# The second layer's attention moved two batches behind the first layer's, with the order of all engines written out in tables

## The reference

```python
x = x + _L0_attn_ref(_layernorm(x), ...)   # 16 heads of 8, softmax attention
x = x + _L0_ffn_ref(_layernorm(x), ...)    # silu(gate) * up, hidden 384, then down
x = x + _L1_attn_ref(_layernorm(x), ...)   # 16 heads of 8, RMS-normed q and k
x = x + _L1_ffn_ref(_layernorm(x), ...)    # base linear + 8 gated experts of rank 8
...
scores = jax.nn.softmax(jnp.einsum('bhse,bhte->bhst', q, k) * scale, axis=-1)
att = jnp.einsum('bhst,bhte->bhse', scores, v)
```

## Time and profile before

| | |
|---|---|
| median of 3 runs | 2082.71 us (2080.16 to 2085.62) |
| the profiled execution, own time | 2080.51 us |
| its span | 2078.7 us |
| TensorE busy | 1806.1 us (87%) |
| VectorE busy | 1601.2 us (77%) |
| ScalarE busy | 1431.7 us (69%) |
| GpSimd busy | 433.7 us (21%) |

### The profile page before, as it was taken

How to read it: one execution, slowest core, us unless ns; L and a number is a source line. 1 busy time by engine, 2 the same in 40 slices (tenths; PEclk the granted TensorE clock), 3 DMA queues, 4 the chain that set the end, 5 groups by cost and what they waited for, 6 DMA issues and landing times.

```text
span 2078.7 us, 32069 instructions
## 1 busy us (share of the span) xinstructions
PE 1806.1 (87%) x10958; PEld 664.0 (32%) x10958; DVE 1601.2 (77%) x3593; ACT 1431.7 (69%) x2921; POOL 433.7 (21%) x570
## 2 busy tenths in 40 slices
PE   4958998999899999999899998989899989999685
PEld 1232333333233333333233333323333332323322
DVE  3537888887788887887888888788888878787371
ACT  2716777776767777786867777776777868676543
POOL 2112121121213122121312212131211312120300
PEclk9957999999899999999999999999999999999867
DMA  5202214050411405041230504032050504121110
GB/s 112 67 17 79 72 39 123 18 144 17 122 40 48 116 20 140 18 123 38 79 88 18 144 17 132 26 108 58 25 137 18 144 17 119 38 60 36 42 42 17
DMA packets 162644, 141.34 MB, mean 68 GB/s; under 512 B 38761, under 2 KB 144050, under 8 KB 162482
## 3 DMA queue, kind: packets, MB, share of 16 engines
q1 hardware_dynamic: 162482, 139.29, 25.2%
HBM read 77.38 MB, written 55.57 MB: 64 GB/s over the span
## 4 chain that ended last, share of the span: by engine, by line
PE 48%; DVE 17%; ACT 13%; DMA 11%; issue 5%; POOL 4%; SPq 3%; DVEq 0%; ACTq 0%; POOLq 0%
PE ps L1127 16%; DVE neg_max L853 10%; PE ps L1112 9%; ACT probs L647 7%; PE ps L1148 6%; PE ps L1102 5%; PE ps L1078 4%; DMA k_stack<-k_rows 3%; DMA rden_all<-rden_rows 3%; PE ps L1191 2%; PE ps L1153 2%; PE ps L1141 2%; DMA k_rows<-kp 2%; DMA rden_rows<-rden 1%; DVE bn L830 1%
## 5 line engine op out<-in xcount | busy, mean ns | idle before, releaser
L853 DVE TENSOR_REDUCE neg_max<-ps 128x1 f32<-128x512 f32 x2048 | 1318.2, 683 | 159.6 <-PE ps L1102 151.4
L647 ACT ACTIVATE probs<-ps 128x512 f32<-128x512 f32 x2048 | 1093.7, 599 | 296.0 <-PE ps L1112 291.5
L1102 PE MATMUL ps<-k_stack,q_stack 48*128 48x512 bf16 x2048 | 700.2, 400 | 80.1 <-DVE neg_max L853 40.1
L1112 PE MATMUL ps<-q_stack,k_stack 50*128 50x512 bf16 x2048 | 654.8, 390 | 64.4 <-ACT probs L647 58.3
L1127 PE MATMUL ps<-probs,v_aug 128*32 128x512 f32 x4096 | 561.8, 621 | 2.5
L1112 PEld LDWEIGHTS ps<-q_stack,k_stack 50*128 50x128 bf16 x2048 | 150.5, 95 | 505.2 <-ACT probs L647 329.8
L1102 PEld LDWEIGHTS ps<-k_stack,q_stack 48*128 48x128 bf16 x2048 | 157.0, 94 | 284.7 <-DVE neg_max L853 220.3
L551 POOL TENSOR_TENSOR o_raw<-o_raw,rden_all 128x512 f32<-128x512 f32 x64 | 81.6, 1275 | 545.8 <-DMA rden_all<-rden_rows 545.8
L1127 PEld LDWEIGHTS ps<-probs,v_aug 128*32 128x32 f32 x4096 | 82.0, 108 | 138.3 <-issue 91.9
L653 ACT ACTIVATE xn<-x,shift,rstd 128x128 f32<-128x128 f32 x192 | 80.6, 486 | 53.0 <-POOL shift L534 53.0
L568 POOL TENSOR_TENSOR ht<-up,gs 128x512 f32<-128x512 f32 x48 | 61.0, 1271 | 254.1 <-ACT up L628 254.1
(11 more groups left out here) (103 smaller groups left out, 1524.6 us busy)
## 6 DMA issues: line engine op xcount, KB each, us to landing
q_stack<-q_rows SPq DMA_DIRECT2D x128, 192.0 KB, 3.8
k_stack<-k_rows SPq DMA_DIRECT2D x128, 192.0 KB, 4.9
rden_all<-rden_rows SPq DMA_DIRECT2D x64, 256.0 KB
q_rows<-qp SPq DMA_DIRECT2D x32, 384.0 KB, 3.3
k_rows<-kp SPq DMA_DIRECT2D x32, 384.0 KB, 3.0
q_rows<-qp SPq DMA_DIRECT2D x32, 256.0 KB, 3.4
k_rows<-kp SPq DMA_DIRECT2D x32, 256.0 KB, 3.2
x_in<-in_L_attn_x SPq DMA_DIRECT2D x16, 256.0 KB, 2.9
```

Source lines behind the costliest of these rows:

```text
L647: act.activation(probs[:, u % RING, :], ps[:, bank_of(l, u), :], ACT.Exp).then_inc(exps, 1)
L853: dve.tensor_reduce(neg_max[l][:, pair // 2, col:col + 1], ps[:, BANKS + bank_of(l, n), :], AX.X, ALU.max, negate=True).then_inc(max_taken, 1)
L1102: pe.matmul(ps[:, BANKS + bank_of(l, m), :], q_stack[l][row:row + KROWS, pair, tok:tok + 128], k_stack[l][row:row + KROWS, pair, :], start ...
L1112: pe.matmul(ps[:, bank_of(l, u), :], k_stack[l][row:row + AROWS, pair, tok:tok + 128], q_stack[l][row:row + AROWS, pair, :], start=True, s ...
```

## The change

`SLOTS` with its X and Y slots is gone. The attentions stand in a list, `ATTENDS`, with no empty place between them, and layer 1 is two batches behind layer 0 instead of one: (0,0), (0,1), (0,2), (1,0), (0,3), (1,1), ... (0,15), (1,13), (1,14), (1,15). Their places are called slots 0 to 31 below. Each engine has a table of half steps for its pieces, relative to a slot, and `GROUPS` says for every batch at which slot a group starts and by how much it is shifted. In the middle of the kernel M1 of batch b stands beside (1,b-1), 16 half steps ahead of where it stood in its slot; since (0,b) is then three slots back, `pr0` has far more than one slot between the end of its attention and itself. M2 stands 8 half steps ahead in its slot. E stands where it stood.

With this the order at the two ends is another one: M1 of batch 0 stands beside (0,1), M2 of batch 0 beside (0,2); M1 of batches 13, 14 and 15 stand beside (1,12), (0,15) and (1,13); P0 of the first batches is packed closer (`P0_fast`); for batches 14 and 15 of layer 1 the second half of the stack is read at half step 63 (`H1_tail`), since the attention before it is of the same layer and reads the stack until then. The same holds for (0,1) and (0,2) at the start.

Buffers follow: `v_aug`, `res` of layer 1 and `o_raw` of layer 0 become double, `rden_all` is shared by the layers, and the ring of probabilities has 12 tiles instead of 16. The `v_aug` buffers are cleared by GpSimd ahead of the loop instead of by VectorE. A piece of several matmuls is now issued as one loop; it stood at one half step before, too.

```diff
-X_PE = ((1, "xt0"), (3, "q0"), (4, "m01"), (5, "k0"), (7, "qt"), (8, "kt"), (11, "pr1"), (12, "m02"), (14, "v1"),
-        (19, "xt3"), (20, "m03"), (21, "rt"), (27, "ct"), (28, "m10"), (29, "out"))
-SLOTS = [("Y", -1)] + [(k, i) for i in range(BATCH + 2) for k in "XY" if (k, i) != ("Y", BATCH + 1)]
-RING = 16
+RING = 12
+ATTENDS = [(0, 0), (0, 1)] + [a for b in range(2, BATCH) for a in ((0, b), (1, b - 2))] + [(1, BATCH - 2), (1, BATCH - 1)]
+PE_AT = {"A": {"m0": -7, "m1": 9, "m2": 25, "m3": 41},
+         "P0": {"xt0": 3, "q0": 7, "k0": 11}, "P0_fast": {"xt0": 3, "q0": 5, "k0": 7}, "V0": {"v0": 15},
...
+         "M2": {"qt": 15, "kt": 17, "v1": 29},
+         "E": {"pr1": 23, "xt3": 39, "rt": 43, "ct": 55, "out": 59}}
...
+M1_EARLY = -16
+M2_EARLY = -8
+GROUPS = []
+for n, (layer, b) in enumerate(ATTENDS):
+    GROUPS.append(("A", (layer, b), n, 0))
+for b in range(1, BATCH):
+    early = b < 3
+    GROUPS.append(("P0_fast" if early else "P0", b, SLOT_OF[0, b - 1], 2 if 2 <= b <= 3 else 0))
+    GROUPS.append(("V0", b, SLOT_OF[0, b] if early else SLOT_OF[0, b - 1] + 1, -12 if early else -8))
+for b in range(2, BATCH):
+    GROUPS.append(("S0", b, max(SLOT_OF[0, b - 2] + (b > 3), b - 2), 0))
+for b in range(BATCH):
+    tight = b in (0, BATCH - 1)
+    beside = (0, 1) if b == 0 else (1, BATCH - 3) if b == BATCH - 1 else (0, BATCH - 1) if b == BATCH - 2 else (1, b - 1)
+    GROUPS.append(("M1", b, SLOT_OF[beside], 0 if tight else M1_EARLY - 2 * (b == BATCH - 2)))
+    GROUPS.append(("M2", b, SLOT_OF[1, b] - 1, 0 if tight else M2_EARLY))
+    GROUPS.append(("H1_tail" if b >= BATCH - 2 else "H1", b, SLOT_OF[1, b] - 1, 0))
+    GROUPS.append(("E", b, SLOT_OF[1, b] + 1, 0))
...
-        v_aug = [sb(f"v_aug{l}", [128, TT, HEADS, 32]) for l in (0, 1)]
+        v_aug = [[sb(f"v_aug{l}{k}", [128, TT, HEADS, 32]) for k in range(l + 1)] for l in (0, 1)]
...
-        rden_all = [sb(f"rden_all{l}", [128, 2, SEQ]) for l in (0, 1)]
+        rden_all = sb("rden_all", [128, 2, SEQ])
```

More of the change, by code:

```diff
@@ L66, in sem_name @@
[L66 to L85, removed]
@@ new lines, in due_table @@
+def due_table(tables):
+    due = {}
+    for group, b, slot, shift in GROUPS:
+        for table in tables:
+            for name, at in table[group].items() if group in table else ():
+                due.setdefault(name, {})[UNITS * slot + shift + at] = b
+    return due
+PE_DUE, ACT_DUE, DVE_DUE, POOL_DUE, SP_DUE = (due_table([t]) for t in (PE_AT, ACT_AT, DVE_AT, POOL_AT, SP_AT))
+PIECES = ("m0", "m1", "m2", "m3", "v0", "xt0", "q0", "k0", "qt", "kt", "v1", "pr1", "xt3", "rt", "ct", "out",
+          "pr0", "xt1", "g0", "u0", "g1", "u1", "g2", "u2", "dn", "xt2", "qka", "qkb")
@@ new lines, with at, piece_order, sem_name @@
+TIMES = range(-UNITS, UNITS * (LAST + 1))
+def at(due, name, t):
+    return due[name][t] if name in due and t in due[name] else None
+def piece_order():
+    before, last = {}, ("v0", 0)
+    for t in TIMES:
+        for name in PIECES:
+            b = at(PE_DUE, name, t)
+            if b is not None:
+                before[name, b] = last
+                last = (name, b)
+    return before
+BEFORE = piece_order()
+def sem_name(name, b):
+    return f"m{b[0]}" if name[0] == "m" else name
+def count(name, b):
+    return 4 * b[1] + int(name[1]) + 1 if name[0] == "m" else b + 1
@@ L143, in need @@
 def need(eng, sem, value):
[L145 to L155, removed]
+    if value > 0:
+        eng.wait_ge(sem, value)
 def build(nc, T, out_dram):
@@ L658, in save_out @@
             def save_out(l, half, b):
[L659 to L661 removed]
+                act.wait_ge(pv, 16 * SLOT_OF[l, b] + 8 * (half + 1))
+                need(act, read[("pr0", "pr1")[l]], b if l == 1 else b - 1)
+                copy(o_of(l, b)[:, half, :], acc).then_inc(o_saved, 1)
             def take(name, dst, b):
@@ L1259, in _ @@
-            walk(pe, slot)
+            pe.wait_ge(first_loaded, 16 * 6)
+            for name in ("xt0", "q0", "k0", "v0"):
+                if name == "xt0":
+                    last = turn_norm(0, 0)
+                elif name == "v0":
+                    pe.wait_ge(read["k0"], 1)
+                    last = by_token(gen4, xnt[0], wv[:, :], range(TT))
+                else:
+                    pe.wait_ge(read["xt0" if name == "q0" else "q0"], 1)
+                    last = pe.matmul(gen, (wq if name == "q0" else wk)[:, :], xnt[0][:, :], start=True, stop=True)
+                last.then_inc(written[name], 1)
@@ new lines, in _ @@
+            weights_turned()
+            for t in TIMES:
+                a = attend_at(t)
+                if a is not None:
+                    attend_score(*a)
+                a = max_at(t)
+                if a is not None:
+                    max_score(*a)
+                a = attend_at(t - 7)
+                if a is not None and a[2] % 4 == 0:
+                    attend_pv(*a)
+                for name in PIECES:
+                    b = at(PE_DUE, name, t)
+                    if b is not None:
+                        parts = PARTS_OF[name] if name in PARTS_OF else 1
+                        for k in range(parts):
+                            last = piece(name, k, b)
+                        last.then_inc(written[sem_name(name, b)], 1)
```

835 lines of the change are left out of this document (401 added, 434 removed), and 20 rows, old and new, of tables (DVE_AT, PIECE, POOL_AT).

## The result

The changed kernel is slower: 2112.26 us median of 4 runs (2104.92 to 2115.24) against 2082.41 of the kernel before on the same chip, a ratio of 1.0137 [1.0108, 1.0166]. The forecast was 1999 us, with a range of 1964 to 2040. The profiled execution took 2111.59 us, its span 2109.8.

What follows compares the result with a forecast made beforehand. No engine was full; the span was cut at exponentials, showing two holes without attention. 2078.7 - 90.1 (holes) + 6 (ends) + 0 (middle) = 1994.6 us span, in the median's terms 1999 us, range 1964 to 2040.

Steps and rivals of the forecast that it cites:

- The holes close: Two stretches without exponentials, 67.0 and 47.4 us, go; their pieces move beside attentions; net -90.1 us.
- The new short paths at the ends: Where same-layer attentions are neighbours, the second's stack is read late: +6 us, from 0 to 28.
- The middle comes to 0 (-2.5 to +3 a pair): Over 12.5 middle slot pairs, gains from M2's lead and costs on ScalarE and VectorE cancel: 0.
- Stack wait -1.4, clock -1.15: In the middle, M2's lead removes TensorE's stack wait, and perhaps the low clock: together -2.55 us a pair.
- ScalarE's crowding and the reads +1.0 (0 to 2): Early in middle layer-0 slots, ScalarE has 3.3 us more reads and parts, partly hidden: +1.0 us a pair.
- Rival B: Packed slot starts cost: TensorE waits on ScalarE, up_mul behind normalise; +3 us a pair, 2037 us; chance 0.17.
- Newton steps +1.6: Twelve VectorE steps of 0.20 us move to bare half steps 47 to 58 of layer-1 slots: +1.6 us a pair.
- M1's move: M1 sixteen half steps ahead in the middle: only its Newton steps were priced, +1.6 us a pair.
- Parts at nothing: Ring of 12 tiles, shared rden_all, GpSimd's clearing and pr0's later place: booked at no cost.
- Rival D: Slower than before: normalise ahead of the first up_mul on GpSimd in 13 layer-1 slots; 2090 us; chance 0.04.
- Slot 28: First of three slots from (0,15) to (1,14) near the end, forecast at about 73 us.
- The clock's price: Half of TensorE's time at the lower clock is lost, 16.1 of 30.5 us in three middle slots.

Runs made afterwards that it cites:

- a lead of 2: Changed kernel with M2 two half steps ahead instead of eight, in four variants of the lead of M1 or its Newton steps: medians 1972.07 to 2007.26 us.
- M2 back: Changed kernel with M2 at its old half steps instead of eight ahead, all else as changed: 2035.9 us, ratio 0.9791 to the kernel before.
- Newton 4: Changed kernel with M1's last twelve Newton steps only four half steps ahead and M2 two ahead: 1999.73 us, ratio 0.9587 to the kernel before.
- Newton 2: Changed kernel with M1's last twelve Newton steps two half steps ahead and M2 two ahead: 1976.12 us, ratio 0.9485 to the kernel before.
- P0 later: Changed kernel with P0 of batches 4 to 15 eight half steps later, M2 still eight ahead: 2072.86 us, ratio 0.9983 to the kernel before.
- parts back and spaced: Changed kernel with M2's bf16 parts, residuals and row DMAs at old half steps, q0 at 5 and k0 at 13: 2051.65 us, ratio 0.9816 to kernel before.

## Why the prediction was wrong, point by point

**The holes close: right.** Both are gone, slot 1 has its 65.7 us, and the kernel with M2 and M1 at their old places shows this part alone: 0.968. Its ends, all outside slots 4 to 27, take 2009.8 - 12 x 119.5 = 576 us, where the forecast's have 1994.6 - 12 x 119.3 = 563. The new short paths at the ends are not what makes the 13 us of difference. In the changed kernel TensorE stood for the stack 1.4 us in slot 0, 2.8 in slot 2 and 4.0 in slots 30 and 31, together 8.2 where 6 were booked. (A wait of 5.9 us for the very first stack stands ahead of all attentions; the kernel before has it too, with 6.6.) The difference is in the slots: with M2 and M1 back slot 0 takes 49.1 us where 44.1 were counted, slot 28 78.9 for 73, slot 29 67.1 for 63.

**The middle comes to 0 (-2.5 to +3 a pair): this step failed,** at +7.8. It was made of four terms; the reads and parts, the clock and the Newton steps were all mis-sized, the first most.

- *Stack wait -1.4, clock -1.15.* The wait went as booked. The clock went the other way: 8.1 us at the low level in a layer-0 slot where there were 2.8, because new waits took the old one's place. The two terms were also not apart: of the 16.1 us that the three slots of the earlier trace rows lost, 5.0 are their longer waits for the stack (2.58, 2.09 and 3.18 us, against 0.96 in the fourth), so 11.1 us are left for 30.5 us of low clock, 0.36 each. That the gain was real the kernels with a lead of 2 show: no low clock in any of their layer-0 slots, and 55.75 to 56.3 us with it.
- *ScalarE's crowding and the reads +1.0 (0 to 2).* Measured against the kernel with M2 back: 5.5 us a pair, 4.0 of it standing, and that with the stack's wait of 1.5 us already saved. I added up what ScalarE has to do in a stretch (3.3 us more) and looked for slack in TensorE to hide it. But what counts is the order in the two queues around one bank: read, piece, read, piece with no scores between them makes the two engines take turns, and neither's spare time is of use. The same holds for the parts, in the queues of ScalarE and GpSimd: part, residual, part, with the exponentials behind them. I had listed `q0` and `qt` at one half step and priced it at 1 us; `m01` between `qt` and `kt`, at the half step of `kt`, I did not see at all, and `kt` waits 1.49 us for its read. Nor did I see the wait of 2.12 us at the parts. Rival B had the place right ("four pieces of q and k within five half steps make TensorE wait on ScalarE three times") but not the parts, and stood at +3 a pair where this part alone measures 5.5.
- *Newton steps +1.6.* Measured 3.3. I took TensorE's pace of 0.65 us a half step as the bound of that stretch, with 0.05 of slack under each maximum's 0.60. The windows rows say otherwise: even without the steps VectorE is busy 10.53 of 10.60 us there, since casts and reciprocals stand between the maxima, so each step counts in full. With them it is 13.07 of 13.10, and the stretch is 2.5 us longer; on the mean of the 12 slots it is 3.0 (13.6 against 10.6). The rest is one step that takes far longer than 0.28 us.

The steps on VectorE in the changed kernel, in the last of these half steps, and what GpSimd does beside them:

```profile
667.10 0.28 DVE L970 TENSOR_TENSOR nw_t<-nw_y 128x128 f32<-128x128 f32 x1
667.30 0.68 DVE L887 TENSOR_REDUCE neg_max<-ps 128x1 f32<-128x512 f32 x1
667.90 0.28 DVE L972 SCALAR_TENSOR_TENSOR nw_u<-nw_t,ms 128x128 f32<-128x128 f32 x1
668.10 0.69 DVE L887 TENSOR_REDUCE neg_max<-ps 128x1 f32<-128x512 f32 x1
668.70 0.76 DVE L975 SCALAR_TENSOR_TENSOR nw_y<-nw_u,nw_y 128x128 f32<-128x128 f32 x1
669.38 3.07 DVE L887 TENSOR_REDUCE neg_max<-ps 128x1 f32<-128x512 f32 x5
...
667.95 1.36 POOL L583 TENSOR_TENSOR o_raw<-o_raw,rden_all 128x512 f32<-128x512 f32 x1 [17.23 <-DMA rden_all<-rden_rows]
```

Step and maximum take 0.80 us together, as in the earlier trace rows, and the last step 0.76 alone. It begins while GpSimd's `normalise` runs, and ends 0.15 us behind it (669.46 against 669.31). In each of the 12 layer-1 slots of the middle one step does so, and takes 0.76 to 1.34 us; that adds 0.8 us a slot, and with twelve steps at 0.20 nearly the whole of the 3.3. Maxima that begin during a `normalise` are not longer (52 of them, 0.69 us at most). With the steps at their old place no step meets a `normalise`, nor does one in the kernel before. "Newton 4" has one again in each slot (0.80 to 1.30 us for a step of 0.22), which is 0.8 of its 1.5 us. In "Newton 2" none is longer, and it loses 0.1. I had priced the steps against the maxima and not looked at GpSimd.

**M1's move** was booked as nothing but these steps. Nearly right: without them the layer-1 slots take 60.5 to 60.7 us, where they take 61.3 with M1 back. M1's lead is a gain of 0.6 to 0.8 us a slot that its own last twelve instructions turned into a loss. (The step from 62.3 before to 61.3 came with M1 and M2 at their old places.)

**Parts at nothing: right for the ring,** which costs nothing by its own run. For the shared denominators and GpSimd's clearing no run stands; nothing of them shows in the middle, where the kernel with both back takes 119.5 us a pair as before (119.3).

**Rival D** (`normalise` ahead of the first `up_mul` on GpSimd) put the change on the right side by the wrong mechanism. In the changed kernel VectorE waits for `ht` 5 times, 6.0 us in total, in the whole middle. What could lose was the term with the factor of 12, and its bound of +3 a pair was drawn from sums of busy time, which cannot show such waits.

**Slot 28** took 85.1 us for 73 forecast. With M2 back it takes 76.8, so 8.3 of the 12 are M2's place again; it has TensorE wait once 2.8 us for m_parts and once 2.8 for `gs`. The rest isn't settled. One cause is in the sum: M2 with E was priced as 55.4 us at a clock of 1.00 over a bare slot of 41.7 us that ran at 0.90. That slot has 0.10 x 2 x 41.7 = 8.3 us of low clock in it, at 0.35 to 0.5 each 3 to 4 us, by which the 12.0 came out low (an estimate from these rows).

**The clock's price** of a half is an upper figure here. The changed kernel and the one with P0 later have about the same idle time in a layer-0 slot (9.7 and 9.1 us), 8.1 and 0.5 us at the low level, and lengths of 63.2 and 59.2: 4.0 less, 3.4 of it for 7.6 us of low clock, 0.45 each. Within the changed kernel the comparison is cleaner: four layer-0 slots with 3.4 us of low clock take 61.5 us, seven with 10.2 take 63.9, at 10.0 and 9.6 us of idle time, so 0.35 each. And 0.36 is what the prediction's own three slots give without their waits. The Trainium skill (TensorE: Matmul & The Clock Gate, Terms) gives throttled time times (1 - K/N), here 3.8. The 3.4 across the two kernels comes near it, the 0.35 within one kernel does not, and there the measurement decides.

## What to carry to other kernels

A stretch with little to do on each engine isn't free for pieces that pass through one bank: write down the two queues side by side and see whether two reads follow each other with no other work between them, and what stands ahead of each read. Before small instructions are moved to a bare stretch, read each engine's busy time in a window of just that stretch; VectorE at 99% there makes every one of them count in full. Look also at what GpSimd does in that window: a step of 0.28 us that began beside its `normalise` took up to 1.34. And where a gain has two parts, as the holes and the lead here, try the least lead that removes the wait: 2 half steps gave all that 8 had been meant to give, and together with the steps' old place 1972 us instead of 2112.

## What was not expected of the hardware

TensorE's clock does not follow its idle time. In layer-0 slots it was low for 8.1 us at 9.7 us of standing, for 0.5 at 9.1, for 7.9 at 6.2 ("parts back and spaced"), for 5.0 at 5.7 and not at all at 5.5 to 5.9 (M2 two half steps early). The ring of 16, with the waits of the changed kernel, had 5.6 instead of 8.1, so a difference of 2 or 3 us says little.

Where the falls begin, the traces do show. In the changed kernel one begins at the wait of 1.49 us for m_parts, or within 1.5 us behind it, in all 12 slots, and a second one in the same way at the wait of 2.12 us in 8 of them. In "parts back and spaced" one begins so at the stack's wait, 1.3 to 3.2 us long, in 10 of 12. But a wait alone doesn't decide it: with P0 later the same 1.49 us stand in each of the 12 slots, and a fall begins there in one. What makes the difference isn't settled; no run here separates it. So in this kernel the clock's part of a change of order (8.1 us at 0.35 to 0.5 each, 3 to 4 us a slot) could be read after the fact and not be worked out ahead.

Nor was it expected that a small VectorE instruction would wait for GpSimd: in the changed kernel all 13 Newton steps that began during a `normalise` ended 0.15 us behind it, at 0.76 to 1.34 us instead of 0.28.
